# Retention scores: one group of twelve 32-row matmuls on unstacked q and k, and denominators clipped in PSUM

## What is computed

```python
q = (xf @ Wq.T).reshape(B, L, H, KD).transpose(0, 2, 1, 3)
k = (xf @ Wk.T * SCALING).reshape(B, L, H, KD).transpose(0, 2, 1, 3)
qr = theta_shift(q, sin_q, cos_q)
kr = theta_shift(k, sin_k[None, None], cos_k[None, None])
qk = jnp.einsum('bhqd,bhkd->bhqk', qr, kr) * mask[None]
den = jnp.clip(jax.lax.stop_gradient(jnp.abs(qk)).sum(-1, keepdims=True), 1.0, 50000.0)
qk = qk / den
out = jnp.einsum('bhqk,bhkd->bhqd', qk, vr).transpose(0, 2, 1, 3)
```

## Time and profile before

| | us |
|---|---|
| median of 3 runs | 2471.46 (2471.05 to 2474.01) |
| the profiled execution | 2479.87 |
| its span, first to last instruction | 2478.1 |
| of it layer 0, to about | 1031 |

### The profile page before, as it was taken

The page is one execution under the profiler, slowest core; times in us unless marked ns, Lnnn a source line. Parts: engine busy times, 40 slices in busy tenths (PEclk is TensorE's granted clock), DMA queues, the critical chain, the costliest instruction groups (busy, mean ns, idle before and its releaser), DMA issues.

```text
span 2478.1 us, 36390 instructions
## 1 busy us (share of the span) xinstructions
PE 2437.3 (98%) x13326; PEld 1688.8 (68%) x13326; DVE 1855.7 (75%) x2772; ACT 1464.8 (59%) x2063; POOL 999.8 (40%) x695
## 2 busy tenths in 40 slices
PE   8999999999999999999999999999999999999999
PEld 4444444444444444699899878888888888888887
DVE  5888888888888888777777667777666667767775
ACT  3676767676767676666666455555555555555554
POOL 3787777777777777314332301111111100111110
PEclk9999999999999999999999989999999999999999
DMA  7222323232323233244454340000000000000000
GB/s 250 51 78 68 86 69 86 69 86 69 86 69 85 69 86 87 73 66 91 75 93 82 52 111 26 26 26 26 26 26 26 26 26 26 17 17 19 26 26 17
DMA packets 117058, 149.91 MB, mean 60 GB/s; under 512 B 32769, under 2 KB 74121, under 8 KB 116625
## 3 DMA queue, kind: packets, MB, share of 16 engines
q1 hardware_dynamic: 116352, 146.87, 23.5%
q10 hardware_dynamic: 528, 0.72, 0.1%
HBM read 71.93 MB, written 25.26 MB: 39 GB/s over the span
## 4 chain that ended last, share of the span: by engine, by line
PE 89%; DVE 6%; issue 2%; ACT 1%; DMA 1%; POOL 0%; SPq 0%; DVEq 0%; POOLq 0%
PE scores L445 10%; PE scores L1766 9%; PE scores L1768 9%; PE scores L1767 9%; PE pairC L458 8%; PE pairC L475 6%; PE pairD L379 3%; DVE l_prod L586 3%; PE pairC L1766 2%; PE pairC L1767 2%; PE pairC L1768 2%; PE pairD L1766 2%; PE pairD L1768 2%; PE pairD L1767 2%; PE pairD L388 2%
## 5 line engine op out<-in xcount | busy, mean ns | idle before, releaser
L586 DVE TENSOR_TENSOR l_prod<-scores,l_window 128x1024 f32<-128x1024 f32 x512 | 613.6, 1217 | 142.2 <-PE scores L445 134.3
L799 ACT ACTIVATE l_absp<-l_prod 128x1024 f32<-128x1024 f32 x512 | 540.2, 1056 | 293.4 <-DVE l_prod L586 283.6
L445 PE MATMUL scores<-l_qst,l_kst 96*128 96x512 f32 x1024 | 380.9, 462 | 14.0 <-DVE l_prod L586 10.9
L1925 ACT ACTIVATE e_r<-scores,e_bn,e_rs 128x512 f32<-128x512 f32 x256 | 197.9, 779 | 276.7 <-PE scores L1768 276.6
L2156 POOL TENSOR_TENSOR e_xnorm<-e_res,e_scale 128x1024 f32<-128x1024 f32 x16 | 38.5, 2404 | 775.9 <-DMA e_res<-t2T_scratch 775.9
L445 PEld LDWEIGHTS scores<-l_qst,l_kst 96*128 96x128 f32 x1024 | 164.9, 190 | 272.9 <-DVE l_prod L586 132.1
L915 POOL TENSOR_TENSOR l_absp<-l_absp,l_absp 128x1024 f32<-128x1024 f32 x126 | 297.8, 2384 | 14.3 <-ACT l_absp L799 14.0
L2032 DVE CAST e_h1hi<-e_r 128x512 fp32r<-128x512 f32 x256 | 144.0, 563 | 208.2 <-ACT e_r L1925 207.9
L1935 ACT ACTIVATE e_r<-scores,e_bn,e_rs 128x512 f32<-128x512 f32 x250 | 195.1, 781 | 138.8 <-PE scores L1768 137.3
L458 PE MATMUL pairC<-l_prod,l_v 128*32 128x512 f32 x2048 | 268.1, 595 | 0.5 <-ACT l_tA L803 0.5
L2059 DVE TENSOR_TENSOR e_r<-e_r,e_wbc 128x512 f32<-128x512 f32 x250 | 170.9, 690 | 86.2 <-ACT e_r L1935 85.9
(11 more groups left out here) (249 smaller groups left out, 4982.8 us busy)
## 6 DMA issues: line engine op xcount, KB each, us to landing
l_kst<-l_hi SPq DMA_DIRECT2D x248, 64.0 KB, 2.0
l_qst<-l_hi SPq DMA_DIRECT2D x248, 64.0 KB, 2.0
l_xo<-in_x SPq DMA_DIRECT2D x32, 256.0 KB, 3.0
x_scratch<-l_xo SPq DMA_DIRECT2D x32, 256.0 KB, 2.4
l_xa<-x_scratch SPq DMA_DIRECT2D x8, 1024.0 KB, 8.2
l_xr<-x_scratch SPq DMA_DIRECT2D x8, 1024.0 KB, 5.5
t2T_scratch<-l_xt SPq DMA_DIRECT2D x8, 1024.0 KB, 14.9
e_scale<-rows_scratch SPq DMA_DIRECT2D x16, 512.0 KB, 4.1
```

The source lines that it names most:

```text
L445: mm = nc.tensor.matmul(sc[j][:, s, :], kst[g][0:96, h, 128 * kt:128 * kt + 128], qst[c][0:96, h, :], start=True, stop=True)
L586: nc.vector.tensor_tensor(prod[2 * (S % 2) + j][:], sc[j][:], win[:, 4 * g + 2 * j:4 * g + 2 * j + 2, w0:w0 + QC], ALU.mult).then_inc(prod ...
L799: nc.scalar.activation(absp[S % ABS][j][:], prod[2 * (S % 2) + j][:], ACT.Abs).then_inc(abs_ready, 1)
L1925: nc.scalar.activation(r1[:, m, :], p1[m], ACT.Relu, bias=bn_[0][1][:, m, n:n + 1], scale=rs[0][:, m, n:n + 1]).then_inc(r1_ready, 1)
```

## The change

The stacks go: `qst`, `kst`, `hi`, `lo`, all the DMAs that filled them and the waits on them. ACT and POOL write the high and low parts straight into `qhi`, `qlo` (one pair for each half of the queries) and `khi`, `klo` (one pair for each group of heads), where the four heads lie on the four groups of 32 partitions. The scores of a step are one group of twelve matmuls in place of four: for each of the three terms, four matmuls with 32 rows each, one head each, each head in its own PSUM bank, the three terms summed there. The group is issued whole at the start of the iteration and waits for both products of the step before; there is one signal for all four heads. In DVE's order both products of a step stand together and its side work behind them. The denominators are scaled in place in PSUM, then clipped from PSUM into `dent`, and the bank counts as free after the clip (`den_ready`) in place of after the scaling. The second half of the window is loaded as soon as the first high part of k is there. Places in memory move; layer 1 changes only in the name of that semaphore.

```diff
-    hi, lo = sb("hi", [128, QC], F32R), sb("lo", [128, QC], F32R)
-    kst = [sb(f"kst{g}", [128, 4, L], F32R) for g in range(2)]
-    qst = [sb(f"qst{c}", [128, 4, QC], F32R) for c in range(2)]
+    khi, klo = ([sb(f"{n}{g}", [128, L], F32R) for g in range(2)] for n in ("khi", "klo"))
+    qhi, qlo = ([sb(f"{n}{c}", [128, QC], F32R) for c in range(2)] for n in ("qhi", "qlo"))
...
         sp.wait_ge(first_hi, K0 + 1)
-        first_stack(sp, K0, (0, 2), range(4))
...
-        first_stack(sp, K1, (1,), range(4))
         sp.dma_start(win[:, H // 2:H], window[:, H // 2:H]).then_inc(window_in, 16)
...
-            if has_q(P):
-                stack(prep_q(P), qst[(P + 1) % 2][:, :, :], QUADS["q"], q_stacked)
...
-            if has_kv(P):
-                stack(prep_k(P), kst[(P // 2 + 1) % 2][:, :, QC * (P % 2):QC * (P % 2) + QC], QUADS["k"], k_stacked[P % 2])
...
-                pe.wait_ge(den_scaled, before[1] + 1)
+                pe.wait_ge(den_ready, before[1] + 1)
...
-        def scores(S, j):
+        def scores(S):
...
-            if kt == 0 and j == 0:
-                pe.wait_ge(q_stacked, STACK * (P + 1))
-            if c == 0 and kt % 4 == 0 and j == 0:
-                pe.wait_ge(k_stacked[kt // 4], STACK * (P // 2 + 1))
+            if P == 0 and kt == 0:
+                pe.wait_ge(first_lo, Q0 + 1)
+            elif P == 0 and kt == 4:
+                pe.wait_ge(first_lo, K1 + 1)
+            elif kt == 0:
+                pe.wait_ge(lo_ready, prep_q(P - 1) + 1)
+            elif kt == 4 and c == 0:
+                pe.wait_ge(lo_ready, prep_k(P - 1) + 1)
             if S > 0:
-                pe.wait_ge(prod_ready, 2 * S + j - 1)
-            for s in range(2):
-                h = 2 * j + s
-                mm = nc.tensor.matmul(sc[j][:, s, :], kst[g][0:96, h, 128 * kt:128 * kt + 128], qst[c][0:96, h, :],
-                                      start=True, stop=True)
+                pe.wait_ge(prod_ready, 2 * S)
+            for n, (k, q) in enumerate(((khi, qhi), (klo, qhi), (khi, qlo))):
+                for h in range(4):
+                    rows = slice(32 * h, 32 * h + 32)
+                    mm = nc.tensor.matmul(sc[h // 2][:, h % 2, :], k[g][rows, 128 * kt:128 * kt + 128], q[c][rows, :],
+                                          start=(n == 0), stop=(n == 2))
             mm.then_inc(scores_ready, 1)
...
         for S in range(KT * PHASES):
             for part in range(2):
-                if S + 1 < KT * PHASES:
-                    scores(S + 1, part)
+                if S + 1 < KT * PHASES and part == 0:
+                    scores(S + 1)
                 side_tasks(S // KT, S % KT, part)
...
-            dve.wait_ge(scores_ready, 2 * S + j + 1)
+            dve.wait_ge(scores_ready, S + 1)
...
-            nc.vector.tensor_tensor(dent[:], nT_A[:, :, 0], scales[:, 0, P % 4, :], ALU.mult).then_inc(den_scaled, 1)
+            nc.vector.tensor_tensor(nT_A[:, :, 0], nT_A[:, :, 0], scales[:, 0, P % 4, :], ALU.mult).then_inc(den_scaled, 1)
             dve.wait_ge(den_scaled, P + 1)
-            nc.vector.tensor_scalar(dent[:], dent[:], 1.0, 50000.0, ALU.max, ALU.min).then_inc(den_ready, 1)
+            nc.vector.tensor_scalar(dent[:], nT_A[:, :, 0], 1.0, 50000.0, ALU.max, ALU.min).then_inc(den_ready, 1)
...
             products(S, 0)
+            products(S, 1)
             if kt == 3 and P > 0:
                 centre(P - 1)
...
                 statistics(b + 1, (1,))
-            products(S, 1)
...
-        def high(n, stacks, count):
-
-            if stacks is not None:
-                act.wait_ge(stacks, count)
+        def high(n):
+
             act.wait_ge(sum_ready, n + 1)
-            nc.scalar.activation(hi[:], t1[:], ACT.Copy).then_inc(hi_ready, 1)
+            nc.scalar.activation(prepared(n)[0], t1[:], ACT.Copy).then_inc(hi_ready, 1)
```

More of the change, by code:

```diff
@@ L39, in memory_map @@
     row(32 * K, *((f"l0_prod{n}", 4 * K) for n in range(4)))
-    row(48 * K, *((f"l0_qst{c}", 8 * K) for c in range(2)))
-    row(64 * K, ("l0_kst1", 16 * K), ("l0_window", 60 * K), ("l0_kst0", 16 * K))
+    row(48 * K, ("l0_qhi0", 2 * K), ("l0_qlo0", 2 * K), ("l0_qhi1", 2 * K), ("l0_qlo1", 2 * K))
+    row(64 * K, ("l0_khi1", 4 * K), ("l0_klo1", 4 * K))
+    row(80 * K, ("l0_window", 60 * K), ("l0_khi0", 4 * K), ("l0_klo0", 4 * K))
     row(156 * K, ("l0_raw", 8 * K), ("l0_xn", 8 * K), ("l0_cos", 4 * K), ("l0_sin", 4 * K))
@@ L230, in layer0, with prepared @@
     NMADE = 3
[L232 to L250, removed]
+    def prepared(n):
+        if n % 2 == 0:
+            c = (n // 2 + 1) % 2
+            return qhi[c][:], qlo[c][:]
+        P = n // 2
+        g, part = (P // 2 + 1) % 2, slice(QC * (P % 2), QC * (P % 2) + QC)
+        return khi[g][:, part], klo[g][:, part]
     r.xo_out, r.prod_ready, r.n_taken, r.d_taken, r.den_done = xo_out, prod_ready, n_taken, d_taken, den_done
-    r.den_scaled, r.o_added, r.centred, r.idn = den_scaled, o_added, centred, idn
+    r.den_ready, r.o_added, r.centred, r.idn = den_ready, o_added, centred, idn
     r.PHASES, r.STEPS, r.UNITS, r.OUTS = PHASES, KT * PHASES, len(units), len(o_order)
@@ L269, in sync @@
             sp.dma_start(dst, src).then_inc(consts, 16)
[L271 to L281, removed]
-        sp.wait_ge(first_hi, K0 + 1)
-        first_stack(sp, K0, (0, 2), range(4))
[L285 to L291, removed]
-        first_stack(sp, K1, (1,), range(4))
+        sp.wait_ge(first_hi, K0 + 1)
         sp.dma_start(win[:, H // 2:H], window[:, H // 2:H]).then_inc(window_in, 16)
@@ L498, in tensor @@
         busy(6)
-        scores(0, 0)
-        scores(0, 1)
+        scores(0)
         pe.wait_ge(consts, 16 * NCONST)
@@ L863, in scalar @@
             if kt == 2 and has_q(P):
-                high(prep_q(P), *(stacks_before_q(P) if P else (k_stacked[0], STACK)))
+                high(prep_q(P))
             if kt == 3 and P > 0:
@@ L867, in scalar @@
             if kt == 6 and has_kv(P):
-                high(prep_k(P), *stacks_before_k(P))
+                high(prep_k(P))
             after.early_scalar(act, PHASES - P, kt)
@@ L899, in rotated, with low @@
             nc.gpsimd.tensor_tensor(t1[:], t1[:], t2[:], ALU.add).then_inc(sum_ready, 1)
-        def low(n, stacks, count):
-            if stacks is not None:
-                pool.wait_ge(stacks, count)
+        def low(n):
             pool.wait_ge(hi_ready, n + 1)
-            nc.gpsimd.tensor_tensor(lo[:], t1[:], hi[:].bitcast(F32), ALU.subtract).then_inc(lo_ready, 1)
+            high, low = prepared(n)
+            nc.gpsimd.tensor_tensor(low, t1[:], high.bitcast(F32), ALU.subtract).then_inc(lo_ready, 1)
         def group_rstd(b):
@@ L951, in gpsimd @@
                 rotated(prep_q(P))
-                low(prep_q(P), *(stacks_before_q(P) if P else (k_stacked[0], STACK)))
+                low(prep_q(P))
             add_pair(KT * P + 2, 0)
@@ L962, in gpsimd @@
             if has_kv(P):
-                low(prep_k(P), *stacks_before_k(P))
+                low(prep_k(P))
             after.early_gpsimd(pool, PHASES - P)
```

23 lines of the change are left out of this document (7 added, 16 removed).

## The result

The changed kernel takes 2481.61 us (median of 7 runs, 2479.48 to 2484.91), the kernel before in the same rounds 2473.35 (7 runs, 2471.05 to 2478.21). The ratio is 1.0034, 95% interval 1.0023 to 1.0045: 8.3 us slower, where 24 were forecast. The profiled execution has a span of 2479.6 us.

A forecast was written before the change was run, and what follows sets the result against it. PE was taken to set nearly all iterations from phase 4 on. First batch -2.2 us and seven batches +26.5 (+3.8 each) made +24 on the 2471.5 median: 2495 us, range 2462 to 2542.

The forecast's parts named there:

- DVE's side work: On DVE beside the scores: up to about 1.05 us free per step; beyond that, side work lengthens the iteration.
- group_mean: DVE side work in p = 1, iteration 5: takes 1.79 us, making the iteration 3.99 in place of 3.46, 0.53 more.
- The sign: Whole kernel: slower, +24 us in all; chances 0.77 slower, 0.08 same, 0.15 faster.
- The price of a round: Scores on PE: a round of four row tiles costs one matmul, 0.23 us, and the group of three rounds 0.80.
- Rounds overlap in part: Rival, scores on PE: a round takes 0.30 us, the group grows by 0.21, total 2540 us; chance 0.15.
- loads one after the other: Rival, scores on PE: twelve 128-column loads run in turn, 1.6 us, the group doubles, total 2689 us; chance 0.11.
- The change of tiling: PE going from row tiles to the full array: 0.18 us each, leaving 0.05 us of the saving, booked as nothing.
- The faster rival: Rival, PE-set iterations: tiling change hidden, each of 121 saves up to 0.3 us, total 2462; chance 0.15.
- The new chain: Scores and products of a step no longer staggered: their times add up, no iteration under 3.41 us.
- The stall of the projection of k: PE waits for the bank until the clip is done: 0 to 0.18 us, taken as 0.07 in each phase.
- The denominators: Clip L610 on DVE: 1.93 us falls to 0.16 from PSUM; otherwise exposed in the new order, iteration 3 at 4.97.
- The start: First batch: waits for the first stack and `raw` and slow matmuls go, short iterations cost more, -2.2 us net.

The follow-up runs named there:

- The order alone: The kernel before, stacks and clip from SBUF kept, with the changed kernel's order of scores and products: 2521.34 us, ratio 1.0189.
- the run with one term: The changed kernel with only hi times hi of the three score terms: 2408.77 us in one execution.
- The doubled shuffle: The changed kernel with each shuffle of q and k done twice: 2504.07 us, ratio 1.0119.
- with the clip in SBUF: The changed kernel with denominators scaled into SBUF and clipped there, as before: 2490.26 us, ratio 1.0064.
- the staggered kernels with the clip in PSUM: The kernel before with the clip from PSUM: 2472.43 us; with window and second sums also moved: 2463.60; with clip between iteration 3's products too: 2453.62.
- the second profile of before: The kernel before, unaltered, run and profiled once more: 2475.96 us, ratio 1.0002; its profiled execution took 2474.39 us.

## Why the prediction was right and wrong

24 us were forecast and 8 measured. The step that failed most is "DVE's side work lies between products(S, 1) and products(S+1, 0), beside the scores, so up to about 1.05 us of it is free": the slack is larger behind an iteration that PE makes long. It accounts for 1.3 of the 3.0 us by which the forecast of a batch was too high (3.8 against 0.8). The rest is group_mean, sized wrong (0.56), iteration 3 (0.7), the other iterations that PE sets (0.4) and iteration 6 of p = 1 (0.26), less 0.2 the other way.

- **The sign** was right: the gain on PE is eaten by a change of tiling and by the end of the stagger. The order alone makes the kernel 1.9% slower, and row tiles and clip win back 1.5%.
- **The price of a round**, 0.23 us: right (0.23 in the timeline, 0.235 by the run with one term). "Rounds overlap in part" and "loads one after the other", 0.26 of the chances, are out. Four loads of 128 columns on the four groups of rows take 0.19 us together in the changed kernel, where eight on the full array took 1.09. The prediction said of the page that it leaves this open, which goes for the section it named alone: the Trainium skill, TensorE: Matmul & The Clock Gate, The mechanism, says that loads overlap running matmuls when the groups of rows differ, and the trace agrees.
- **The change of tiling**, 0.18 us: it measures about 0.1, but the group with the change, 0.98 forecast, is 0.90, and an iteration that PE sets is 0.03 to 0.04 shorter. "Nothing booked" was nearly right; over 121 iterations it is 4 us. The faster rival needed 0.2. (Its own 33 us are 0.27 for each iteration, not the 0.3 written beside them.)
- **The new chain**, 3.41 us: 3.43 measured. From the first score to the products it is 1.02 us (537.19 to 538.21), 0.99 forecast. It alone gave p = 0, iteration 5, +0.44 forecast and +0.45 measured, and most of p = 3, iterations 4 and 5.
- **DVE's side work**: this step failed. I worked out DVE's own path rightly: 3.67 us with a shuffle, and 3.65 in the rows (530.98 to 533.95, and 0.68). But I compared it with 3.43, the length of the iteration in which the shuffle is written. The products before it start in iteration 0, whose 3.81 us PE sets; 3.67 is under that. Slack isn't a constant 1.05 us for each step: behind an iteration that PE sets it is larger by what that iteration is over 3.43: 0.4 behind iteration 0, 1.2 behind 3. The doubled shuffle showed this. By cases: iteration 1 +0.24 each, measured +0.02; p = 2, iteration 1 +0.95, measured +0.53; the shuffle in iteration 4 of p = 3, +0.26 of the 1.01, measured nothing (+0.80 for iterations 4 and 5, the chain's part). Where no long iteration of PE stood ahead, the size was right: p = 2, iteration 2 +0.17, measured +0.24. Iteration 2 of p = 0 grew by 0.11, which no step had.
- **The stall of the projection of k**, +0.07 in each phase: none measured. For p = 0 the clip ends 0.91 us after the products (541.47 against 540.56), where 1.04 was forecast, and the projection starts 1.05 after them (541.61), 0.90 us behind the scores as elsewhere. The gain in p = 2 was forecast as 0.38 and is 0.68.
- **The denominators**: L610's 1.93 us went to 0.175, near the low bound of 0.16. That it "would be exposed in the new order", an iteration of 4.97 us, was wrong: with the clip in SBUF, iteration 3 is at most 4.83 us in batches 1 to 6. That the sum of these, 31 iterations of some 0.3 us, is near the 8.7 us measured, is luck, since half of the 8.7 stands in the last two phases.
- **Group_mean**, +0.53 in p = 1, iteration 5, measured -0.03: taken as 1.79 us from its rows, it is 1.17 now. Its 1.14 us at L643 were a wait, not a cost: in the staggered kernels with the clip in PSUM, too, L643 takes 0.16 us and iteration 5 of p = 1 falls from 3.46 to 3.10. I had read L610 as such a wait and didn't ask the same of L643. The slack behind iteration 4, 4.05 us long here, would have hidden nearly all of the 1.79 as well (from 579.45; the scores let the products start at 581.22). Iteration 6 of p = 1 went from 5.00 to 4.74; no step had it.
- **The start**, -2.2 us for the first batch: -3.8 measured, and with it an error of several us, since the first stall differs between executions of one kernel.
- **Layer 1**, 0: up to 3 us, open.

The sum again, against the second profile of before: first batch -3.8, batches 1 to 6 +4.8, last +2.5, layer 1 +3.5, together 7.0. Forecast: -2.2 + 26.5. The forecast is over it by 19.2 us in the seven batches and by 1.6 at the start, and under it by 3.5 in layer 1, which brought the total nearer by luck.

## What to carry to other kernels

When two engines take turns, don't compare an engine's work in a step with that step's length before: write down for each step what either engine needs and what the other one has left over from the step ahead; only what is over both is a loss. A saving can be won in some iterations and lost in others to a wait that it brings with it (the clip), or stay hidden until another engine's work is moved away, so look at it iteration by iteration and try the two together. And before giving up a stagger, price it: here the order without it cost 48 us on stacks, more than the 31 that row tiles, no stacks and the earlier window brought in that order.

## What the runs showed of the hardware

- Four row tiles of 32 rows with 512 columns, loads of 128 columns included, take 0.235 us, as one matmul of the full array does. The Trainium skill, TensorE: Matmul & The Clock Gate, Measured speedup vs the span model, would give 0.30, an estimate from its 3.07; here the measurement decides.
- A change from row tiles to the full array costs about 0.1 us, an estimate from the 0.43 us of one round up to the projection, less 0.235 and the start of 0.11. The Trainium skill, TensorEngine Tiling (Array Packing), Key Properties, says that such a change drains the engine; the trace agrees, in that a cost is left, and it is small.
- Some small DVE instructions from SBUF to SBUF end just when POOL's instruction ends. In the second profile of before these are POOL and then DVE:

```profile
581.08 1.29 POOL L899 TENSOR_TENSOR l_t<-l_t,l_t 128x512 f32<-128x512 f32 x1
```

```profile
581.25 1.14 DVE L643 TENSOR_TENSOR l_gvar<-l_mv,l_dmean 128x2 f32<-128x2 f32 x1
```

POOL ends at 582.37, DVE at 582.39; two columns took 1.14 us. L610 there runs from 542.43 to 544.37, and the first of POOL's two additions of 128x1024 (4.72 us for both, from 541.95) ends at about that time. All 7 of L643 and 30 of the 32 of L610 end so, within 0.07 us if POOL's two additions are equally long. The two others, here the first of them in the profile of before, started before POOL's instruction, and took 0.17 us with their input in SBUF:

```profile
1008.12 0.17 DVE L610 TENSOR_SCALAR l_den_t<-l_den_t 128x16 f32<-128x16 f32 x1
```

```profile
1008.23 4.77 POOL L915 TENSOR_TENSOR l_absp<-l_absp,l_absp 128x1024 f32<-128x1024 f32 x2 [8.56 <-ACT l_absp L799]
```

With its input in PSUM the same clip takes 0.175 us, also while POOL's additions run (in the changed kernel from 540.68, the clip at 541.29). The Trainium skill, VectorE: DVE Perf Modes, Why PSUM operands drop a tier, says that one mode of DVE needs both of its ports for reading SBUF and that it has only one for PSUM; that the clip is freed by input in PSUM agrees. That POOL holds one of the two is my inference; the runs show the times.
- Single executions of one kernel differ by 1.4 us (before) and 4.5 us (changed) by the start of layer 1, with waits for `raw` of 4.46 and 2.42 us in the two of before, and by 4.1 and 1.7 us in layer 1.
